# Area attention with a query chunk outermost, pair sums on GpSimd, and three maximum banks

## The reference

```python
# layer 0: x = x + bn(proj(out + pe)); qkv = bn(conv1x1(groupnorm(x)))
Ba, Na = (B * AREA, N // AREA)            # 16 areas of 1024 pixels
qkv = qkv.reshape(Ba, Na, NUM_HEADS, 3 * HEAD_DIM).transpose(0, 2, 3, 1)   # 8 heads of 32
q, k, v = (qkv[:, :, :HEAD_DIM], qkv[:, :, HEAD_DIM:2 * HEAD_DIM], qkv[:, :, 2 * HEAD_DIM:])
attn = jnp.einsum('bhdn,bhdm->bhnm', q, k) * scale
attn = jax.nn.softmax(attn, axis=-1)
out = jnp.einsum('bhdm,bhnm->bhdn', v, attn)
# pe = bn(depthwise 7x7 conv(v)); then layer 1: a modulated deformable 3x3 convolution
# of groupnorm(x), 256 to 256 channels, added to x
```

## Time and profile before

| what | value |
|---|---|
| median of 3 executions | 5446.0 us (5424.45 to 5457.83) |
| profiled execution, its own time | 5460.12 us |
| its span, first to last instruction | 5458.3 us |
| mean granted TensorE clock, share of full speed | 0.91 |
| PE / DVE / POOL / ACT busy over the span | 4297.0 / 3864.0 / 3276.5 / 2382.9 us |
| instructions | 77391 |

### The profile page before, as it was taken

The page is one execution under the profiler, slowest core; times in us unless marked ns, Lnnn a source line. Parts: engine busy times, 40 slices in busy tenths (PEclk is TensorE's granted clock), DMA queues, the critical chain, the costliest instruction groups (busy, mean ns, idle before and its releaser), DMA issues. The chain is left out here.

```text
span 5458.3 us, 77391 instructions
## 1 busy us (share of the span) xinstructions
PE 4297.0 (79%) x18884; PEld 1811.5 (33%) x18884; DVE 3864.0 (71%) x6758; ACT 2382.9 (44%) x4441; POOL 3276.5 (60%) x1968
## 2 busy tenths in 40 slices
PE   1888888888888888888838988577878787778777
PEld 0222222222222222222216664323434343444333
DVE  5887887887887887888710027128888888888887
ACT  1355555555555555555420015324444444444444
POOL 0476676676676666676631111117777777777786
PEclk9799899999899999899878989788999999999999
DMA  4111111111111111111169877869999999999998
GB/s 155 37 52 39 44 47 45 52 54 37 44 46 46 51 56 36 44 48 44 32 152 191 181 185 289 227 170 368 375 359 368 356 360 357 368 356 360 366 352 329
DMA packets 372161, 966.30 MB, mean 177 GB/s; under 512 B 53281, under 2 KB 160417, under 8 KB 355281
## 3 DMA queue, kind: packets, MB, share of 16 engines
q0 software_dynamic: 165888, 604.05, 29.2%
q1 hardware_dynamic: 205904, 358.24, 23.1%
HBM read 805.78 MB, written 104.96 MB: 167 GB/s over the span
## 5 line engine op out<-in xcount | busy, mean ns | idle before, releaser
L402 POOL TENSOR_TENSOR psum<-psum,pr 128x1024 f32<-128x1024 f32 x576 | 1494.7, 2613 | 405.4 <-ACT pr L470 396.3
L1365 POOL DMA_INDIRECT gat<-gather_table,idc x1152 | 1367.2, 1187 | 458.5 <-issue 346.0
L514 DVE TENSOR_REDUCE nmx<-mring 128x1 f32<-128x512 f32 x2048 | 1304.1, 681 | 441.5 <-PE mring L645 433.5
L470 ACT ACTIVATE pr<-ering 128x512 f32<-128x512 f32 x2048 | 1150.5, 598 | 1000.6 <-PE ering L665 995.9
L1481 PE MATMUL pac<-smt,wds 128*128 128x512 f32 x2304 | 1099.6, 622 | 26.1 <-ACT smt L1380 26.1
L645 PE MATMUL mring<-ks,qs 96*128 96x512 f16 x2048 | 868.7, 424 | 248.5 <-DVE nmx L514 240.8
L665 PE MATMUL ering<-qs,ks 98*128 98x512 f16 x2048 | 835.8, 416 | 162.4 <-DMA qs<-mlo 123.7
L1380 ACT COPY smt<-ptr 128x512 f32<-128x512 f32 x576 | 335.3, 582 | 854.8 <-PE ptr L1493 854.2
L1433 DVE SCALAR_TENSOR_TENSOR pbb<-gat,wtc,pa 128x256 f32<-128x256 f32 x1152 | 511.8, 479 | 276.6 <-ACT pa L1390 269.0
L1493 PE MATMUL ptr<-cst,sm 128*128 128x128 f32 x2304 | 381.0, 292 | 372.0 <-DVE sm L1447 371.6
L1481 PEld LDWEIGHTS pac<-smt,wds 128*128 128x128 f32 x2304 | 437.8, 200 | 488.4 <-issue 448.4
(11 more groups left out here) (133 smaller groups left out, 3092.7 us busy)
## 6 DMA issues: line engine op xcount, KB each, us to landing
toep<-toe SPq DMA_DIRECT2D x64, 896.0 KB, 10.7
gather_table<-pix SPq DMA_DIRECT2D x64, 512.0 KB, 8.4
va<-v_pixel_major SPq DMA_DIRECT2D x40, 512.0 KB, 7.7
gat<-gather_table,idc POOLq DMA_INDIRECT x1152, 6.2
xs<-xa SPq DMA_DIRECT2D x16, 1024.0 KB, 4.8
xin<-xa SPq DMA_DIRECT2D x16, 1024.0 KB, 4.9
qs<-qkh SPq DMA_DIRECT2D x256, 64.0 KB, 2.0
ks<-qkh SPq DMA_DIRECT2D x256, 64.0 KB, 2.0
```

The lines of the kernel that those rows point to most:

```text
L402: gp.tensor_tensor(psum[:, g, h, :], pr[:, 0, h, :] if m == 1 else psum[:, g, h, :], pr[:, m % 2, h, :], ALU.add).then_inc(s_pa, 1)
L470: act.activation(pr[:, m % 2, h, c * 512:(c + 1) * 512], ering[n % 2][:, :], ACT.Exp).then_inc(s_e, 1)
L514: dve.tensor_reduce(nmx[:, g, n // CH, n % CH:n % CH + 1], mring[n % 2][:, :], AX.X, ALU.max, negate=True).then_inc(s_mf, 1)
L1365: gp.indirect_dma_start(gat[:, r, :, :].rearrange("p q c -> p (q c)"), None, tab, bass.IndirectOffsetOnAxis(ap=idc[:, e, u:u + 1], axis=0) ...
```

## The change

The two chunks of 512 queries, so far the innermost loop, become the outermost one of a half. A half has the same 32 slots with the same number of score products and exponentials, but a slot holds two heads of one chunk. `weigh` runs once for each of the 16 steps (chunk, key tile) into one bank `acc`, as often as before.

- **Sums.** POOL adds the weights of two key tiles of all four heads in one instruction of 128x2048 (`add_pair`, eight a half); PE multiplies each pair sum by ones and accumulates four of them per chunk in a bank of its own (`den`): eight groups of four matmuls a half, in every fourth slot, where there were two. DVE adds nothing.
- **Banks.** `mring` has three banks, so a `max_unit` waits for the reduction three before it. The two `wring` banks become one `wbank`.
- **Order on PE.** v tiles and denominators stand between the two score pairs of a slot.
- **DVE to POOL.** `split` and `divide` run on POOL: the splits behind pair sums 4 and 5, the divisions behind 3 and 7. `max_parts` reads PSUM twice and has no `mrow`.
- **Reciprocals.** There are two chains a half (one for each chunk) of `copy_den`, four fold DMAs, `recip`, one DMA out, four DMAs in. DVE's `recip` stands at slot 25 for the half's own first chunk and at slot 10 for the second chunk of the half before.
- **SP's list.** It gets `invert` (fold, wait for DVE, write, spread) and `store_out` for each chunk.

```diff
-                    def add(i, g, m, h):
+                    def add_pair(i, g, k):
+                        gp.wait_ge(s_e, i * (HG * EXN) + (E0 + g * EXN + (k + 1) * 2 * HQ))
...
+                        m = 2 * k % NT
+                        gp.tensor_tensor(psum[:, k % 2, :, :].rearrange("p h n -> p (h n)"),
+                                         pr[:, m, :, :].rearrange("p h n -> p (h n)"),
+                                         pr[:, m + 1, :, :].rearrange("p h n -> p (h n)"), ALU.add).then_inc(s_pa, 1)
...
+                            for k in range(SUMS):
+                                add_pair(i, g, k)
...
+                                if k == Y_SUM[1] and not (first and g == 0):
+                                    divide(*before)
+                                if k == Y_SUM[0]:
+                                    divide(i, g, 0)
+                                if not last and k in QL_SUM:
+                                    split(i + 1, g, QL_SUM.index(k))
```

```diff
+            DEN_AT = 8
+            NUM_SLOT = (SLOTS // CH + 1, 1)
+            DEN_SLOT = (DEN_AT + 4 * (CSUMS - 1) + 1, DEN_AT + 4 * (SUMS - 1) + 1 - SLOTS)
+            R_SLOT = (DEN_SLOT[0] + 4, DEN_SLOT[1] + 5)
+            Y_SUM = (7, 3)
+            QL_SUM = (4, 5)
```

The part of SP's list, and the new function in it:

```diff
+                    def invert(i, g, c):
+                        n = g * CH + c
+                        sp.wait_ge(s_dn, i * (HG * CH) + (n + 1))
                         for h in range(HQ):
+                            sp.dma_start(fold[HD * h:HD * h + HD, :], dnm[HD * h:HD * h + 1, c, :]).then_inc(s_fold, 16)
+                        sp.wait_ge(s_rc, i * (HG * CH) + (n + 1))
                         sp.dma_start(rec_d.rearrange("h (p n) -> (h p) n", p=HD), fold[:, :]).then_inc(s_rs, 16)
...
                         if not last:
                             stack(i + 1, 1 - odd, 0)
+                        invert(i, 0, 0)
                         max_rows(i, odd, 1)
-                        fold_den(i, 0)
-                        spread_recip(i, 0)
+                        store_out(i, 0, 0)
+                        invert(i, 0, 1)
+                        store_out(i, 0, 1)
                         if not last:
                             stack(i + 1, 1 - odd, 1)
+                        invert(i, 1, 0)
+                        if not last:
                             max_rows(i + 1, 1 - odd, 0)
+                        store_out(i, 1, 0)
```

And on PE:

```diff
-                        if n >= 2 or g or not isinstance(j, int) or j:
-                            pe.wait_ge(s_mf, mcount(j, g, n - 1))
-                        pe.matmul(mring[n % 2][:, :], qs2[0:96, odd, g, h, t * P:(t + 1) * P],
+                        if n >= 3:
+                            pe.wait_ge(s_mf, mcount(j, g, n - 2))
...
+                        pe.matmul(mring[n % 3][:, :], qs2[0:96, odd, g, h, t * P:(t + 1) * P],
...
+                                if slot % 4 == 0:
+                                    k = (slot - DEN_AT) // 4
+                                    if k >= 0:
+                                        denominators(i, g, k)
+                                    elif not (first and g == 0):
+                                        denominators(*before, k + SUMS)
+                                pair(1)
```

More of the change, by code:

```diff
@@ L350, in body @@
                             load_x(i + 1)
+                        if not first:
+                            invert(i - 1, 1, 1)
                         sp.wait_ge(s_ve, i * NT + NT)
@@ L371, in _ @@
                     over_areas(sp, body)
-                    fold_den(NA - 1, 1)
-                    spread_recip(NA - 1, 1)
-                    sp.wait_ge(s_yo, NA * HG * CH)
-                    store(ya_d, NA - 1, yo_all, s_out)
-                    sp.wait_ge(s_out, 16 * NA)
+                    invert(NA - 1, 1, 1)
+                    store_out(NA - 1, 1, 1)
+                    for c in range(CH):
+                        sp.wait_ge(s_out[c], 16 * NA * HG)
                     sp.wait_ge(s_vout, 16 * NA)
@@ L405, in body @@
                     def body(i, odd, first, last):
                         for g in range(HG):
-                            for m in range(1, NT):
-                                for h in range(HP):
-                                    add(i, g, m, h)
-                                if m == 1 and g == 0 and not last:
+                            before = (i, 0, 1) if g else (i - 1, 1, 1)
+                            for k in range(SUMS):
+                                add_pair(i, g, k)
+                                if k == 1 and g == 0 and not last:
@@ new lines, in body @@
+                            before = (i, 0, 1) if g else (i - 1, 1, 1)
+                            for slot in range(SLOTS):
+                                step = slot // 2
+                                if slot % 2 == 0 and not (first and g == 0 and step < NT):
+                                    weights_free(i, g, step)
+                                for x in range(2):
+                                    n = slot * 2 + x
+                                    act.wait_ge(s_s, i * (HG * EXN) + (g * EXN + n + 1))
+                                    act.activation(pr[:, step % NT, n % HQ, :], ering[n % 2][:, :],
+                                                   ACT.Exp).then_inc(s_e, 1)
+                                if slot == NUM_SLOT[0]:
+                                    copy_num(i, g, 0)
+                                if slot == DEN_SLOT[0]:
+                                    copy_den(i, g, 0)
+                                if not (first and g == 0):
+                                    if slot == NUM_SLOT[1]:
+                                        copy_num(*before)
+                                    if slot == DEN_SLOT[1]:
+                                        copy_den(*before)
+                                if not last:
+                                    for n in share(slot, *QK_AT, QKN):
+                                        qk_evac(i + 1, g, n)
@@ new lines, in denominators @@
+                    def denominators(i, g, k):
+                        pe.wait_ge(s_pa, i * (HG * SUMS) + (g * SUMS + k + 1))
+                        if k % CSUMS == 0 and (g or k or not isinstance(i, int) or i):
+                            pe.wait_ge(s_dn, i * (HG * CH) + (g * CH + k // CSUMS))
+                        for h in range(HQ):
+                            mm = pe.matmul(den[HD * h:HD * h + HD, :], ones[:, :], psum[:, k % 2, h, :],
+                                           start=k % CSUMS == 0, stop=k % CSUMS == CSUMS - 1,
+                                           tile_position=(0, HD * h))
@@ L706, in body, with pair @@
                             for slot in range(SLOTS):
[L707 removed]
                                 units = list(() if g and last else share(slot, 0, M_END, MXN))
[L710 to L713 removed]
+                                def pair(x):
+                                    scores(i, odd, g, slot * 2 + x)
+                                    if x < len(units):
+                                        max_unit(i + g, odd if g == 0 else 1 - odd, 1 - g, units[x])
+                                pair(0)
                                 if g == 0:
@@ L716, in body @@
                                         v_tile(i, t)
-                                if not (first and g == 0):
-                                    if slot == DSLOT:
-                                        denominators(*before, g and last)
+                                if slot % 4 == 0:
[5 more added lines that the diff above has]
+                                pair(1)
                                 if not last:
@@ L739, in _ @@
                     over_areas(pe, body)
-                    for c in range(CH):
-                        weigh(NA - 1, 1, NT - 1, c)
-                    denominators(NA - 1, 1, True)
+                    weigh(NA - 1, 1, STEPS - 1)
+                    for k in range((SLOTS - DEN_AT) // 4, SUMS):
+                        denominators(NA - 1, 1, k)
         keep = ExitStack()
```

309 lines of the change are left out of this document (120 added, 189 removed).

## The result

The changed kernel takes 5762.2 us (median of 4 runs, 5753.6 to 5782.3) against 5444.8 us before (4 runs): a ratio of 1.0605, 95% interval 1.058 to 1.063. It is slower, as forecast (5740 us, +5.4%). The profiled execution took 5782.3 us, with a span of 5780.5 us.

The account below looks back on a forecast made before the run. A half was bound by PE's work, its stalls behind DVE and the wait at its end, 81.4 us; 55.2 + 36.5 = 91.7 us, 30 x 10.3 = +309, together +292 us: 5740 us, +5.4%, range 5560 to 5920 us.

Parts of the forecast that it names:

- The chain: Slots 24 to 31: pair sum 5, second split, stack, fold, reciprocal and restart in series, 36.5 us instead of 15.0.
- the slow restart: At a half's end PE restarts at 1.2 GHz after its stop, adding 1.5 us to the chain.
- The slots ahead of the chain: Slots 0 to 23 at PE's undisturbed pace: 51.8 us with g = 1, 58.7 us with g = 0.
- DVE's stop: DVE stands from slot 25 until the fold lands at 25.9 us; PE idles for about 20 us.
- The split: POOL's second split behind pair sum 5, taken at 2.0 us; an estimate by ratio made it 3.2 us.
- `mlo`: Maximum part at the half's end, now reading PSUM: 0.3 us instead of 2.35 us, without contention with POOL.
- a slow `mlo`: Without the no-contention rule the half's end arm of 34.0 us would be 36 us, 2 x 30 = 60 us more.
- The rival with 10 slow microseconds: PE stays at 1.2 GHz 10 us into the next half: 96 us a half, 5867 us, chance 0.2.
- v tiles: Eight in slots 0 to 23 of g = 0 add 6.9 us; sharing one bank was costed at nothing.
- Area 15, last half, start: Three corrections outside the 30 stopped halves: area 15 with g = 0 -14 us, last half -10 us, start +7 us.
- The premise that DVE's additions cost their work: DVE loses seven additions of 2.20 us and two splits of 1.62 us, 18.6 us a half.
- The gain of slots 0 to 23: With DVE no longer stalling PE, two slots take 3.31 us; these slots take 55.2 us in the mean.

Follow-up runs that it names:

- e1: The changed kernel with the first chunk's fold, reciprocal and spread ahead of the 24 stack DMAs on SP: 5503.9 us, ratio 1.0104.
- e4: The changed kernel with DVE's reciprocal of the half's own first chunk moved from slot 25 to slot 30: 5664.8 us, ratio 1.0401.
- e2: The changed kernel with both splits behind pair sum 3, maximum rows right behind the stack, first chunk's fold, reciprocal and division in the next half: 5123.4 us.
- e12: The changed kernel with DVE evacuating each v tile behind the slot's first maximum reduction instead of its last: 5690.2 us, ratio 1.0469.
- e7: The kernel before with six of DVE's seven additions a half cut from 1024 to 32 columns: 5320.5 us, ratio 0.9773.
- e9: The kernel before with six of DVE's seven additions a half replaced by 512-column reductions with one SBUF operand: 5285.7 us, ratio 0.9686.
- e8: e2 with the loop over areas written out on PE alone: 5092.9 us, ratio 0.936.
- e11: e2 plus v tiles evacuated behind the slot's first reduction and the area loops of PE, ACT and DVE written out: 5022.3 us, ratio 0.9209.

## Why the prediction was right, and where its terms were off

- **The chain.** Measured from the start of pair sum 5: split done at 6.6 us (forecast 6.7), stack at 21.7 (22.3), reciprocal at 25.7 (26.3), next score at 37.0 (36.0 with the slow restart). A g = 1 half takes 88.5 us, forecast 51.8 + 36.5 = 88.3. The slots ahead of the chain were a little shorter than forecast (51.5 us from the first score at 1034.42 to the start of the next pair sum 5 at 1085.89, forecast 51.8 + 0.5), the chain a little longer; that the two cancel to 0.2 us is luck. e1 to e4 show that this chain, and in it SP's queue behind the late split, makes the loss: with both ends moved, 22 us a half are gone.
- **The cause inside the chain** was put too much on DVE's stop. With the reciprocal moved out of slot 25 (e4), 86.8 us of a g = 1 half remain. The way out through SP's list was blocked as well.
- **The split**, the price without a row: 2.0 us taken, 2.13 us measured. The estimate by the Trainium skill's ratio (GPSIMD Engine Reference, section 3.1) gave 3.2 us, and was too high here; its duration for the addition, 4497 ns, agrees with the pair sum's 4526 ns here (median).
- **`mlo`**: 0.3 us taken, 0.28 us measured, from 2.35 us. It had not decided anything: PE, with the last `weigh` at 1033.42, is later than the rows' DMAs. For the same reason the forecast's 60 us for a slow `mlo` were too many: its 36 us would have replaced PE's 34.5, not 34.0. Nor does the changed kernel test the reason given for 0.3 us, since POOL is idle when its `mlo` runs, and in the kernel before the old form was as fast the one time that POOL was idle:

```profile
178.44 0.21 DVE L529 CAST mhi<-mrow 32x128 f16<-32x128 f32 x1
178.69 0.28 DVE L531 TENSOR_TENSOR mlo<-mrow,mhi 32x128 f16<-32x128 f32 x1
```

e2 does test it: 31 of its 32 `mlo` run beside a pair sum, and all take 0.28 us. The rows also show that not only two-operand forms wait: the cast `mhi` has one SBUF operand and took 0.21 us here, 1.98 us beside POOL.

```profile
1117.75 4.53 POOL L413 TENSOR_TENSOR psum<-pr 128x2048 f32<-128x2048 f32 x1 [2.87 <-ACT pr L510]
...
1120.39 0.28 DVE L565 SCALAR_TENSOR_TENSOR mlo<-wbank,mhi 32x128 f16<-32x128 f32 x1
```

- **The restart at 1.2 GHz**: +1.5 us taken. PE is busy 5.6 us at a granted clock of 0.50, work that takes about 2.8 us at full clock, so some 2.8 us. The rival with 10 slow microseconds did not come; 2.4 GHz was back 5.7 us after the restart.
- **v tiles, "costed at nothing" but for their own 0.86 us**: this step failed. With the bank shared, eight v tiles cost 98.1 - 88.5 = 9.6 us, not 6.9 us; e12 shows that 4.8 us of it come from the evacuation's place on DVE. What is left, 4.8 us, is less than the 6.9 us priced, so both terms were off, in opposite directions. A g = 0 half is 98.1 us where the forecast had 95.2: 15 x 2.9 us = 43 us of the sum.
- **The loop turn** was in no term. In the kernel before, the six halves with a turn took 84.9 us in the mean and the other g = 0 halves 82.9 us, so most of it was covered. PE waits there for the rows' DMA (3.7 us), and that is the cover: in e1 and e4, where PE again starts a half with a wait for these rows (12.67 and 19.32 us in the rows above), the turn costs 0.4 and 1.0 us, and PE's row at the turn names the DMA and no longer "issue". In the changed kernel it lies open: 6 x 4.9 us = 29 us of the sum.
- **Area 15, last half, start**: 69.0 us (forecast 67); 87.7 to 72.8 us from the last half's first score to the next stage, -15 (forecast -10); first score at 185.05 against 181.46, +3.6 (forecast +7).
- **The later stages, costed at nothing**: behind the attention the two profiles have 2664.8 and 2624.7 us, -40 us, with the same code. This hid the two misses above: from the first score to that of the last half +373.7 us (forecast +309 - 14 = +295), start +3.6, end -14.9, later stages -40.1, together +322 us, which is the span's difference. So the halves grew by 79 us more than forecast, and that the total still came near is luck. These stages, whose code is the same, took 2591 to 2628 us in the changed kernel and the ten runs made from it, and 2665, 2639 and 2656 us in the kernel before, e7 and e9. The scatter among like kernels is nearly as large as the difference, but all eleven lie below all three, so it is hardly chance alone. Its cause stays open.
- **Slips in the working.** The chances, as they are written, add up to 1.02, and slower has 0.85 although the forecast's chain alone, all of it slower, has 0.87. The reciprocals of a chunk, 4 heads x 512 queries in float32, are 8 KB, not 4. Neither moves the time.
- **The premise that DVE's additions cost their work** (18.6 us of DVE a half) named the right engine, but about half of an addition's 2.20 us was a wait for POOL and not work: e7 and e9. The gain of slots 0 to 23 was still right, since moving both kinds away from DVE also removes the wait.

## What to carry to other kernels

When work moves to another engine, follow the last instruction that it releases through every queue, in list order: here one split behind a sum on POOL, and one fold behind 24 DMAs on SP, turned 6% less time (e2) into 6% more. Look for the second gate before blaming the first: an engine that stops in one list is often held by the same late transfer in another. And an idle time that a wait covers, here the turn of a loop, comes up at its full price once the wait is gone.

## What the hardware showed that I had not expected

- A two-operand addition of 32 columns on VectorE takes 0.19 us while GpSimd is idle and 1.78 us in the mean beside its instructions (e7); a reduction of 512 columns beside GpSimd's additions takes 0.68 us (e9).
- At the turn of this loop PE issues nothing for 2.3 to 3.0 us in the changed kernel and for 4.6 to 5.5 us in e2, and ACT for 4.1 to 4.6 us in e8, without any wait shown. In the changed kernel and in e2 PE's first matmuls behind it run at half clock (1.94 us instead of 1.06 us for a group); e11, with these loops written out, has a granted clock of 1.00 over the whole stage.
- 24 small DMAs occupy SP's queue 15.1 us, 0.63 us apart (1004.02 to 1019.12 in the changed kernel); the fold behind them starts only then.
